# A graph kernel's edge stage: zeros written by ScalarE instead of GpSimd, target windows at fixed places, and later waits on VectorE and TensorE

## The chip, the cores and the metric

The kernel runs on one core of a Trainium2 chip. The metric is the device time of one execution in microseconds. Engines are named as the profile names them: PE is TensorE, DVE is VectorE, ACT is ScalarE, POOL is GpSimd and SP is SyncE, which here only issues transfers.

## The reference

Two graph networks run on 3,125 nodes of 128 features and 53,125 directed edges, sorted by target node. The first has one costly part, a three-layer network per edge, in both directions, with its sums per node:

```
edge_inputs  = concatenate([x[src], x[dst], edge_features])          # 3*128 wide
edge_states  = w3 @ relu(w2 @ relu(w1 @ edge_inputs + b1) + b2) + b3  # 384 -> 256 -> 256 -> 128
agg          = segment_sum(edge_states, dst)                          # and the same with src and dst exchanged
s1 = gru(x, agg); s2 = gru(agg, s1); s3 = gru(s1, s2); x = layernorm(x + s3)
for l in range(3):                                                    # second network
    X = relu(((1 + eps[l]) * X + segment_sum(X[src], dst)) @ W1[l] + b1[l]) @ W2[l] + b2[l]
x = layernorm(x + X)
```

The second network's segment sum is done as a product with a dense matrix of edge counts (3,125 x 3,125), which the edge stage counts on the way.

## The kernel before

The work has three stages: `edge_stage`, `gru_stage` and `sum_stage`. The change touches the first, which takes most of the time.

The edges are cut into G = 104 groups of 512. Because they are sorted by target, the 512 edges of a group have their targets in a short run of nodes. Each engine has its own program for a group, called a turn, and the engines meet at semaphores.

What a turn does, in the order of the data:

- POOL gathers the rows `x[src]` into `xg` (`gather`, L431), four transfers per group; SP loads the edge features `ef`, a copy of the group's indices in every partition (`rowb`), and a window of 128 node rows `xw`, whose first node `base` is read from a table `base_i` computed in the prologue from the group's smallest target.
- ACT rounds `xw` to `xwh` (`upper`, L573) and DVE takes the rest, `xwl` (L791). DVE makes the one-hot matrix `hot` (L806) and PE forms x[dst] as `xwh * hot + xwl * hot` (L1147, L1148). These two and the transposes of `xg` are `turn_sd`.
- ACT copies the transposed rows to `sd` (L554), DVE forms sum and difference (L786, L787), ACT rounds them (`upper_sd`, L559; `upper_e`, L567, for the features) and DVE takes the lower parts `sdl` (`lower_parts`, L796 and L799).
- PE does the first layer (`first`, L1106), ACT the bias (`pb`, L578), DVE the two directions (`ways`: `hpre`, L769 and L770), ACT the rounding with the relu (`h1h`, L584), DVE the lower parts `h1l` (L775). PE does the second layer (`second`, L1120), ACT its relu (L590), PE the third (`third`, L1131), ACT copies the two results to `es` (L598).
- `total` on PE sums the first direction into the group's window of 128 nodes (L1178, with the one-hot matrices `same[par][:, 0]` of `nodes`, L813) and combines equal indices of the second direction (L1183, with `same[par][:, 1]` of `compare`, L820). DVE adds the first to `aggt` at column `base` (`deliver`, L903). ACT copies the second to `outb` (L608), and POOL adds its rows to a table in HBM (`add`, L438), at places that DVE computes in `places` (L828 to L842).
- Beside this, DVE makes one-hot matrices of the edges' rows and columns (`pair_hot`, L874, L875), PE multiplies them (`pairs_of`, L1162) and DVE adds the counts to a band of the count matrix (`count_pairs`, L885, two halves per group). The `band` is a ring of three blocks of 120 columns; every fourth group one block is complete. SP then writes it to HBM (`flush`), POOL zeroes it (L462) and raises `s_fresh`, for which DVE waits at the head of the turn that will use it again. Every twelfth group DVE folds the ring's overhang back (`wrap`, L891, L893).

The order of instructions on each engine is written out by hand. The 12-turn loops of DVE, POOL and SP run seven rounds from group 8 (10 for SP), with the other groups before and behind them; PE and ACT loop over two turns. The prologue clears `aggt`, `band` and the later stage's `x1` on POOL (L422 to L424), computes per group the smallest and largest target and from these `base_i`, two ring places and a flag `fits`; if every group fits its windows, the windowed program runs, which is the case in the trace, else a general one.

## Time and profile before

| what | value |
|---|---|
| median of 3 runs | 2551.1 us (2547.54 to 2552.36) |
| profiled execution, its own time | 2548.59 us |
| its span in the profile | 2546.7 us |
| mean granted PE clock | 0.965 |
| PE busy | 2328.4 us, 91% of the span |
| DVE busy | 1831.1 us, 72% |
| ACT busy | 1145.7 us, 45% |
| POOL busy | 1269.6 us, 50% |

The own time is 1.9 us above the span, which leaves out what lies around it. The span falls into four stretches: the prologue to 42 us, the 104 groups from 42 to about 2050 us, the recurrent layers to 2223 us, and the three sum layers to the end. Busy shares tell little here, since PE is busy in most of every stretch; what matters is by how much a group takes longer than its PE work.

### The profile page before, as it was taken

The numbers are of one execution on the slowest core, as the hardware profiler recorded it, in microseconds if no ns is written. First come the engines' busy times: TensorE is split into PE (matmuls) and PEld (weight loads), VectorE is DVE, ScalarE is ACT, GpSimd is POOL, SyncE is SP. The second block draws the span as 40 slices with busy tenths as digits, with TensorE's granted clock in tenths as the row PEclk, the third lists the DMA queues.
The fourth block names the chain that finished last, engine by engine and source line by source line (L and its number), as shares of the span: only waits on it lengthen the run. The fifth ranks groups of instructions, "written<-read, shape, count | busy, mean of one in ns | idle before, by whom it ended". The sixth has DMA issues, their size and how long they took to land. (4 is left out here: it accounts for less than half of the span.)

```text
span 2546.7 us, 43212 instructions
## 1 busy us (share of the span) xinstructions
PE 2328.4 (91%) x12735; PEld 1942.8 (76%) x12735; DVE 1831.1 (72%) x3624; ACT 1145.7 (45%) x2031; POOL 1269.6 (50%) x873
## 2 busy tenths in 40 slices
PE   3999998999999999999999999999999949799997
PEld 2888787888778877878787788788887835478886
DVE  8888887888788877878887788778888836611114
ACT  1555555455455545545555455455555504311112
POOL 4566566666566666665665566556666410000000
PEclk9999999999999999999999999999999979899999
DMA  4356555355555355554355453555543462086963
GB/s 139 77 117 120 98 91 96 75 93 101 93 95 92 79 94 92 97 103 81 76 107 91 90 91 83 90 91 96 102 89 76 68 155 98 26 358 234 392 253 152
DMA packets 238770, 296.04 MB, mean 116 GB/s; under 512 B 125755, under 2 KB 196286, under 8 KB 230220
## 3 DMA queue, kind: packets, MB, share of 16 engines
q1 hardware_dynamic: 165449, 240.46, 33.9%
q0 software_dynamic: 73216, 54.58, 16.6%
q14 instruction: 89, 0.73, 0.1%
q8 instruction: 16, 0.26, 0.0%
HBM read 221.91 MB, written 73.05 MB: 116 GB/s over the span
## 5 line engine op out<-in xcount | busy, mean ns | idle before, releaser
L438 POOL DMA_INDIRECT sums<-outb,target x416 | 695.5, 1672 | 645.6 <-ACT outb L608 416.3
L431 POOL DMA_INDIRECT xg<-in_x,gidx x416 | 493.1, 1185 | 151.6 <-issue 135.8
L590 ACT ACTIVATE h<-ebank,b2c 128x512 f32<-128x512 f32 x416 | 286.7, 691 | 343.5 <-PE ebank L1120 343.5
L1131 PEld LDWEIGHTS ebank<-w3t,h 128*128 128x128 f32 x3328 | 403.9, 192 | 13.4
L1131 PE MATMUL ebank<-w3t,h 128*128 128x128 f32 x3328 | 404.7, 275 | 0.0
L1120 PE MATMUL ebank<-h1h,w2h 128*128 128x512 f32 x832 | 369.9, 445 | 3.9 <-DVE h1l L775 3.9
L1120 PE MATMUL ebank<-h1h,w2l 128*128 128x512 f32 x832 | 329.6, 396 | 0.0
L1120 PE MATMUL ebank<-h1l,w2h 128*128 128x512 f32 x832 | 329.2, 396 | 0.0
L584 ACT ACTIVATE h1h<-hpre 128x512 fp32r<-128x512 f32 x416 | 237.8, 622 | 125.8 <-DVE hpre L770 125.8
L1106 PE MATMUL ebank<-sdh,w1h 128*128 128x512 f32 x624 | 255.7, 410 | 39.0 <-DVE sdl L796 34.8
L775 DVE SCALAR_TENSOR_TENSOR h1l<-hpre,h1h 128x512 fp32r<-128x512 f32 x416 | 258.8, 679 | 0.0
L578 ACT ACTIVATE pb<-ebank,b1c 128x512 f32<-128x512 f32 x208 | 143.3, 689 | 245.1 <-PE ebank L1106 245.1
L1106 PE MATMUL ebank<-sdh,w1l 128*128 128x512 f32 x624 | 251.3, 403 | 0.0
L1106 PE MATMUL ebank<-sdl,w1h 128*128 128x512 f32 x624 | 249.9, 401 | 0.0
L875 DVE TENSOR_SCALAR colhot<-spots,colkey 128x500 bf16<-128x500 f16 x416 | 202.8, 487 | 0.0
L1120 PEld LDWEIGHTS ebank<-h1h,w2h 128*128 128x128 f32 x832 | 160.6, 193 | 38.7 <-DVE h1l L775 4.3
L1120 PEld LDWEIGHTS ebank<-h1h,w2l 128*128 128x128 f32 x832 | 158.6, 191 | 37.4
L1106 PEld LDWEIGHTS ebank<-sdh,w1h 128*128 128x128 f32 x624 | 121.3, 194 | 78.6 <-DVE sdl L796 41.2
L1120 PEld LDWEIGHTS ebank<-h1l,w2h 128*128 128x128 f32 x832 | 160.2, 193 | 25.4
L1178 PE MATMUL ebank<-same,es 128*128 128x128 f32 x832 | 119.0, 289 | 56.7 <-ACT es L598 56.7
L885 DVE TENSOR_TENSOR band<-band,ebank 128x500 f32 x208 | 139.9, 672 | 41.0 <-issue 31.3
L903 DVE TENSOR_TENSOR aggt<-aggt,ebank 128x128 f32 x104 | 30.0, 289 | 187.6 <-PE ebank L1178 125.8
(250 smaller groups left out, 4117.3 us busy)
## 6 DMA issues: line engine op xcount, KB each, us to landing
ring<-adj SPq DMA_DIRECT2D x54, 1568.0 KB, 8.1
rowb<-along SPq DMA_DIRECT2D x104, 512.0 KB
adj<-band SPq DMA_DIRECT2D x25, 1500.0 KB, 13.9
ef<-in_edge_attr SPq DMA_DIRECT2D x103, 256.0 KB, 2.7
stay<-adj SPq DMA_DIRECT2D x6, 1568.0 KB, 14.4
xg<-in_x,gidx POOLq DMA_INDIRECT x416
xw<-in_x SPq DMA_DIRECT2D x104, 64.0 KB
sums<-outb,target POOLq DMA_INDIRECT x416
```

The lines of the kernel that those rows point to most:

```text
L431: pool.indirect_dma_start(out=to, out_offset=None, in_=a["x"], in_offset=bass.IndirectOffsetOnAxis(ap=ids, axis=0)).then_inc(s_x[par], 16)
L438: pool.indirect_dma_start(out=tables[k % 2], out_offset=bass.IndirectOffsetOnAxis(ap=target[par][:, 1, k:k + 1], axis=0), in_=outb[par][:, ...
L578: nc.scalar.activation(pb[:, f, :], bank[2 + 2 * f][:, :], ACT.Identity, bias=b1c[:, f:f + 1]).then_inc(s_pc, 1)
L584: nc.scalar.activation(h1h[:, way, f, :], hpre[:, f, way, :], ACT.Relu).then_inc(s_h1, 1)
L590: nc.scalar.activation(h2[:, way, f, :], bank[6 + f][:, :], ACT.Relu, bias=b2c[:, f:f + 1]).then_inc(s_h2, 1)
L775: nc.vector.scalar_tensor_tensor(out=h1l[:, way, f, :], in0=hpre[:, f, way, :], scalar=0.0, in1=h1h[:, way, f, :].bitcast(fp32), op0=ALU.m ...
L875: last = nc.vector.tensor_scalar(colhot[:, t, :], spots[:, 0:WIDE], of(colkey, t), None, ALU.is_equal)
L885: nc.vector.tensor_tensor(part, part, bank[4 + half][:, 0:WIDE].rearrange("p (b c) -> p b c", c=WIN), ALU.add).then_inc(s_acc, 1)
L1106: last = nc.tensor.matmul(bank[bk + 2 * f][:, :], w[:, f, j, :], x[:, j, :], start=(q == 0), stop=(q == len(parts) - 1))
L1120: last = nc.tensor.matmul(bank[6 + f][:, :], w[:, f, k, :], h[:, way, k, :], start=(q == 0), stop=(q == len(parts) - 1))
L1131: last = nc.tensor.matmul(bank[6 + way][:, t * P:(t + 1) * P], h2[:, way, k, t * P:(t + 1) * P], w3t[:, k, :], start=False, stop=(t == K - ...
L1178: last = nc.tensor.matmul(bank[0][:, 0:P], es[:, 0, t * P:(t + 1) * P], same[par][:, 0, t, :], start=(t == 0), stop=(t == K - 1))
```

## The change

1. **Zeros.** POOL's three memsets of the prologue and its memset of a band block every fourth group go. DVE makes one row of 380 zeros (`none`). ACT copies it, broadcast, to `band`, `aggt` and `x1` at its start, and in the loop it clears a third of a block (25 x 40 columns) in each of the three turns before the block is used again, between `upper` and `first`. For this ACT's loop becomes one of 12 turns, and POOL's, which has no events any more, one of 2 turns. `s_fresh` counts thirds.
2. **Fixed windows.** Group g's window of target nodes begins at `30 g - 16` (clamped at both ends) and is 80 wide (`SPAN`), in place of a computed place and 128. `base_i` shrinks to the two ring places (`slot_i`); SP and DVE no longer load a base from it. `hot`, `xw`, `xwh`, `xwl` use 80 partitions, the node matrices (`into`) 80 columns, L1178 80 moving columns. `fits` also asks that every group's targets lie in its window.
3. **Order and waits.** In DVE's turn `nodes` comes ahead of the first `count_pairs`, the wait for `s_fresh` stands behind `sums` and `nodes`, the second `count_pairs` stands behind `lower_parts`, the wrap stands behind it and one turn earlier, and `places` stands ahead of `deliver`. PE waits for the counts (`s_acc`) ahead of the second half of `first` only.

```diff
-            nc.gpsimd.memset(aggt[:, :], 0.0)
-            nc.gpsimd.memset(band[:, :], 0.0).then_inc(s_band, 1)
-            nc.gpsimd.memset(later.x1[:, :, :], 0.0).then_inc(later.s_zero, 1)
...
-                    if event:
-                        i, b = event
-                        pool.wait_ge(s_flush, i * 16)
-                        plain()
-                        nc.gpsimd.memset(band_of(slots(b), slots(b) + BLK), 0.0).then_inc(s_fresh, 1)
...
+                def clear(i, b, third):
+
+                    act.wait_ge(s_flush, i * 16)
+                    lo = slots(b) + third * (BLK // 3)
+                    nc.scalar.copy(band_of(lo, lo + BLK // 3), none[:, 0:BLK // 3].unsqueeze(1)
+                                   .broadcast_to([P, NB, BLK // 3])).then_inc(s_fresh, 1)
+
...
+                    if cleared:
+                        clear(*cleared)
                     if ahead:
                         first(g + 1)
...
+                    with act.Fori(0, ROUNDS) as m:
+                        for q in range(12):
+                            turn(m * 12 + (8 + q), q % 2, m * 6 + (4 + q // 2),
+                                 cleared=(m * 3 + (2 + q // 4), q // 4, q % 4 - 1) if q % 4 else None)
...
+            nc.scalar.copy(band[:, :].rearrange("p (b c) -> p b c", c=BAND),
+                           none[:, :].unsqueeze(1).broadcast_to([P, NB, BAND])).then_inc(s_band, 1)
...
-                    base = dve.value_load(base_i[0:1, bass.ds(g * 4, 1)], min_val=0, max_val=N - P)
-                    part = aggt[:, bass.ds(base, P)]
-                    nc.vector.tensor_tensor(part, part, bank[0][:, 0:P], ALU.add).then_inc(s_agg, 1)
+                    part = aggt[:, bass.ds(first_node(g), SPAN)]
+                    nc.vector.tensor_tensor(part, part, bank[0][:, 0:SPAN], ALU.add).then_inc(s_agg, 1)
 
                 def turn(g, par, turns, ahead=2, early=0, fresh=None, wrapped=None):
+                    begin = isinstance(g, int) and g == 0
+                    if ahead:
+                        sums(g + 1)
+                    if begin:
+                        pair_keys()
+                        pair_hot(0)
+                    if ahead:
+                        nodes(g + 1, 1 - par, early=early == 2)
                     if fresh is not None:
                         dve.wait_ge(s_fresh, fresh)
-                    if ahead:
-                        sums(g + 1)
-                    if isinstance(g, int) and g == 0:
-                        pair_keys()
-                        pair_hot(0)
-                    if wrapped is not None:
-                        dve.wait_ge(s_acc, g * 2)
-                        wrap(wrapped)
-                    if not (isinstance(g, int) and g == 0):
+                    if not begin:
                         count_pairs(g, 0)
                     if ahead:
-                        nodes(g + 1, 1 - par, early=early == 2)
-                    if not (isinstance(g, int) and g == 0):
-                        count_pairs(g, 1)
-                    if ahead:
                         lower_parts(g + 1)
...
+                    count_pairs(g, 1)
+                    if wrapped is not None:
+                        dve.wait_ge(s_acc, g * 2 + 2)
+                        wrap(wrapped)
+                    if ahead:
+                        compare(g + 1, 1 - par, turns + par)
                     if ahead == 2:
                         onehot(g + 2, par, turns + 1)
                         window(g + 2, par)
                     if ahead:
                         pair_hot(g + 1)
                         ways(g + 1)
+                        places(g + 1, 1 - par, early=early == 2)
                     deliver(g)
-                    if ahead:
-                        places(g + 1, 1 - par, early=early == 2)
```

The first place is DVE's program inside its loop, from the add of the sums to `compare`. The names are those of the list above; `s_aT` says that PE has the pair products, `s_acc` that a half was counted. Before:

```order
L786 TENSOR_TENSOR sd<-sd,ebank 128x512 [waits s_sdT]
L787 TENSOR_TENSOR sd<-sd,ebank 128x512
...
L885 TENSOR_TENSOR band<-band,ebank 128x25x20
L813 ISA [waits s_sum]
L813 TENSOR_TENSOR same<-column,inwin 128x512
...
L885 TENSOR_TENSOR band<-band,ebank 128x25x20
L795 REGISTER_ALU
L796 TENSOR_TENSOR sdl<-ebank,sdh 128x512 [waits s_hi]
L799 TENSOR_TENSOR sdl<-sd,sdh 128x1024 [waits s_hi]
L820 ISA [waits s_rowb0]
L820 TENSOR_TENSOR same<-rowb,keys 128x512
```

The same place of the changed kernel, whose line numbers are some 30 higher (L816 is L786 of before, L915 is L885, L826 and L829 are L796 and L799, L850 is L820):

```order
L816 TENSOR_TENSOR sd<-sd,ebank 128x512 [waits s_sdT]
L817 TENSOR_TENSOR sd<-sd,ebank 128x512
L843 ISA [waits s_sum]
L843 TENSOR_TENSOR into<-column,inwin 128x320
...
L915 TENSOR_TENSOR band<-band,ebank 128x25x20
L825 REGISTER_ALU
L826 TENSOR_TENSOR sdl<-ebank,sdh 128x512 [waits s_hi]
L829 TENSOR_TENSOR sdl<-sd,sdh 128x1024 [waits s_hi]
...
L915 TENSOR_TENSOR band<-band,ebank 128x25x20
L850 ISA [waits s_rowb0]
L850 TENSOR_TENSOR same<-rowb,keys 128x512
```

One count has moved from ahead of the lower parts to between them and the comparison, and the node matrix is narrower.

The second place is the end of DVE's turn, behind `ways`. Before:

```order
L775 SCALAR_TENSOR_TENSOR h1l<-hpre,h1h 128x512 [waits s_h1]
L901 ISA [waits s_agg,s_sum]
L901 TENSOR_LOAD base_i
L901 ISA x2
L903 ISA
L903 TENSOR_TENSOR aggt<-aggt,ebank 128x128
L828 TENSOR_TENSOR match<-same,lower 128x512 [waits s_cmp]
...
L842 TENSOR_TENSOR target<-shift,keys 128x4 [waits s_cs]
```

And in the changed kernel:

```order
L805 SCALAR_TENSOR_TENSOR h1l<-hpre,h1h 128x512 [waits s_h1]
L858 TENSOR_TENSOR match<-same,lower 128x512 [waits s_cmp]
...
L871 REGISTER_ALU [waits s_add1,s_add0]
L872 TENSOR_TENSOR target<-shift,keys 128x4 [waits s_cs]
L932 ISA [waits s_agg,s_sum]
L932 TENSOR_TENSOR aggt<-aggt,ebank 128x80
```

The target computation now stands ahead of the delivery, with its wait for POOL's adds (`s_add0`, `s_add1`), and the load of a base is gone.

The third place is ACT's program in its new loop, in a turn that clears a third of a block; before, the turn had the same rows without the clear.

```order
L573 CAST xwh<-xw 80x128 [waits s_sdT]
L612 ISA
L614 COPY band<-none 128x25x40 [waits s_flush]
L578 ACTIVATE pb<-ebank,b1c 128x512 [waits s_p]
L577 REGISTER_ALU
L578 ACTIVATE pb<-ebank,b1c 128x512 [waits s_p]
```

The clear stands between the window's rounding and the first layer's bias.

## Rows read from the trace of the kernel before

**Rows 1.** Windows, L1147 to next: length, PE, PEld, DVE, ACT, POOL, clock, DMA.
```profile
98.84:116.58 17.74, 17.74 (x110) 15.15 (x108) 15.03 (x32) 10.15 (x18) 10.66 (x9) 1.00 0.38 79
169.76:191.62 21.86, 19.57 (x109) 16.68 (x108) 18.02 (x33) 10.03 (x18) 15.73 (x10) 0.92 0.85 170
284.47:304.35 19.88, 18.28 (x109) 14.99 (x108) 16.01 (x33) 10.13 (x18) 10.75 (x8) 1.00 0.52 95
322.08:342.45 20.37, 17.95 (x110) 15.18 (x108) 18.12 (x32) 10.04 (x18) 12.95 (x9) 1.00 0.34 68
435.33:459.31 23.98, 19.79 (x109) 16.01 (x108) 14.94 (x32) 10.02 (x18) 10.40 (x8) 0.93 0.49 81
```

**Rows 2.** One line, once per group: PE's first product of `turn_sd`; first and last start.
```profile
L1147 PE MATMUL ebank<-hot,xwh x104: 474/478/776, 42.0 to 2019.6; 128*128 128x512 f32 x104
```

**Rows 3.** One line: POOL's memset of a band block, min/median/max in ns.
```profile
L462 POOL MEMSET band<- x24: 3188/3195/3203, 177.6 to 1954.0; 128x3000 f32 x24
```

**Rows 4.** Timeline of DVE while a memset runs (177.59 to 180.8): start, length.
```profile
177.25 3.58 DVE L874 TENSOR_SCALAR rowhot<-spots,rowkey 128x128 bf16<-128x128 f16 x1
```

**Rows 5.** Waits of PE: for whom, us in total, times, longest.
```profile
PE ebank L1178 <- ACT es L598: 56.7, 24, 2.5
```

**Rows 6.** Window right behind such a wait; the number behind POOL's is PE's clock.
```profile
186.00:190.00 4.00, 3.63 (x18) 3.54 (x19) 2.29 (x5) 1.00 (x3) 1.89 (x1) 0.61 1.13 145
```

**Rows 7.** Timeline of the prologue.
```profile
2.86 13.36 DVE L674 CAST column<-count_i 128x128 f32<-128x128 int32 x1 [0.43 <-POOL lower L420]
...
3.87 0.25 SPq L251 DMA_DIRECT2D pb<-in_dst  x1
...
13.38 2.76 POOL L424 MEMSET x<- 128x3200 f32 x1
...
17.79 0.69 DVE L689 CAST hpre<-pb 104x1024 f32<-104x1024 int32 x1
...
34.93 0.30 ACT L573 CAST xwh<-xw 128x128 fp32r<-128x128 f32 x1 [4.76 <-DMA xw<-in_x]
```

**Rows 8.** Transfers of the first 45 us: count, size, us to landing.
```profile
ef<-in_edge_attr SPq DMA_DIRECT2D x3, 256.0 KB, 2.6
```

**Rows 9.** Timeline of one group, from the lower parts to `total`.
```profile
365.42 1.21 DVE L799 TENSOR_TENSOR sdl<-sd,sdh 128x1024 fp32r<-128x1024 f32 x1
...
367.77 0.69 ACT L578 ACTIVATE pb<-ebank,b1c 128x512 f32<-128x512 f32 x1 [0.51 <-PE ebank L1106]
...
369.94 0.67 DVE L769 TENSOR_TENSOR hpre<-pb,ebank 128x512 f32<-128x512 f32 x1
...
373.49 0.57 ACT L598 COPY es<-ebank 128x512 f32<-128x512 f32 x1
...
374.24 0.97 PEld L1178 LDWEIGHTS ebank<-same,es 128*128 128x128 f32 x8
...
374.55 0.59 ACT L598 COPY es<-ebank 128x512 f32<-128x512 f32 x1 [0.49 <-PE ebank L1131]
```

**Rows 10.** First `es` and L1178 in another group.
```profile
1013.64 0.57 ACT L598 COPY es<-ebank 128x512 f32<-128x512 f32 x1
...
1014.88 0.97 PEld L1178 LDWEIGHTS ebank<-same,es 128*128 128x128 f32 x8
```

**Rows 11.** Timeline at the DVE loop's second round: ACT's last copy, then DVE's first work.
```profile
433.86 0.59 ACT L608 COPY outb<-ebank 128x512 f32<-128x512 f32 x1 [1.32 <-PE ebank L1183]
...
441.57 0.69 DVE L786 TENSOR_TENSOR sd<-sd,ebank 128x512 f32<-128x512 f32 x1 [5.58 <-issue]
```

**Rows 12.** Timeline of DVE in a turn with a wrap.
```profile
286.95 0.67 DVE L891 TENSOR_TENSOR band<-band 128x500 f32<-128x500 f32 x1
...
289.16 0.68 DVE L885 TENSOR_TENSOR band<-band,ebank 128x500 f32 x1 [0.89 <-DVE band L893]
```

**Rows 13.** Groups of instructions: busy us, mean ns.
```profile
L559 ACT CAST sdh<-sd 128x1024 fp32r<-128x1024 f32 x104 | 110.1, 1059 | 17.1 <-DVE sd L787 17.1
L1178 PE MATMUL ebank<-same,es 128*128 128x128 f32 x832 | 119.0, 289 | 56.7 <-ACT es L598 56.7
```

More of the change, by code:

```diff
@@ L57 @@
 ROUNDS = 7
+PACE = 30
+BACK = 16
+SPAN = 80
+NB_A = 16
 assert G == 4 * ITERS and WIDE <= 512
@@ L127, in edge_stage @@
         rowb = [sb(f"rowb{i}", [P, 2, GE]) for i in range(2)]
-        same = [sb(f"same{i}", [P, 2, K, P]) for i in range(2)]
+        same = [sb(f"same{i}", [P, K, P]) for i in range(2)]
+        into = [sb(f"into{i}", [P, K, SPAN]) for i in range(2)]
+        none = sb("none", [P, BAND])
         target = [sb(f"target{i}", [P, 3, K], i32) for i in range(2)]
@@ L470, in windowed @@
                 for j in range(1, 8):
-                    turn(j, j % 2, j // 2, event=(1, -1) if j == 6 else None)
-                with pool.Fori(0, ROUNDS) as m:
-                    for q in range(12):
-                        turn(m * 12 + (8 + q), q % 2, m * 6 + (4 + q // 2),
-                             event=(m * 3 + (2 + q // 4), q // 4) if q % 4 == 2 else None)
-                for j in range(8 + 12 * ROUNDS, G + 1):
-                    turn(j, j % 2, j // 2, gathers=("last" if j == G - 3 else j < G - 3),
-                         event=(j // 4, j // 4 - 2) if j % 4 == 2 and j // 4 < ITERS - 1 else None)
+                    turn(j, j % 2, j // 2)
+                with pool.Fori(4, (G - 4) // 2) as i:
+                    for par in range(2):
+                        turn(i * 2 + par, par, i)
+                for j in range(G - 4, G + 1):
+                    turn(j, j % 2, j // 2, gathers=("last" if j == G - 3 else j < G - 3))
                 for t in range(2):
@@ L641, in program @@
                 first(0)
[L642 to L648 removed]
+                if win:
+                    for g in range(8):
+                        turn(g, g % 2, g // 2, early=g < 2, cleared=(1, -1, g % 4 - 1) if g > 4 else None)
+                    with act.Fori(0, ROUNDS) as m:
+                        for q in range(12):
+                            turn(m * 12 + (8 + q), q % 2, m * 6 + (4 + q // 2),
+                                 cleared=(m * 3 + (2 + q // 4), q // 4, q % 4 - 1) if q % 4 else None)
+                    for g in range(8 + 12 * ROUNDS, G):
+                        turn(g, g % 2, g // 2, ahead=min(2, G - 1 - g),
+                             cleared=(g // 4, g // 4 - 2, g % 4 - 1) if g % 4 and g // 4 < ITERS - 1 else None)
+                else:
+                    turn(0, 0, 0, early=True)
+                    turn(1, 1, 0, early=True)
+                    with act.Fori(1, (G - 2) // 2) as i:
+                        for par in range(2):
+                            turn(i * 2 + par, par, i)
+                    turn(G - 2, 0, 0, ahead=1)
+                    turn(G - 1, 1, 0, ahead=0)
+            act.wait_ge(s_none, 1)
+            nc.scalar.copy(band[:, :].rearrange("p (b c) -> p b c", c=BAND),
+                           none[:, :].unsqueeze(1).broadcast_to([P, NB, BAND])).then_inc(s_band, 1)
+            nc.scalar.copy(aggt[:, :].rearrange("p (b c) -> p b c", c=AW // NB_A),
+                           none[:, 0:AW // NB_A].unsqueeze(1).broadcast_to([P, NB_A, AW // NB_A])).then_inc(s_band, 1)
+            nc.scalar.copy(later.x1[:, :, :], none[:, 0:D].unsqueeze(1).broadcast_to([P, NB, D])).then_inc(later.s_zero, 1)
             act.wait_ge(s_wload, 6 * 16)
@@ L1095, in _, with first @@
             pe.wait_ge(s_fits, 1)
-            def first(g, start=False):
+            def first(g, start=False, pairs=False):
                 if not start:
```

98 lines of the change are left out of this document (48 added, 50 removed).

## The prediction

> **What bounds the kernel now.** The busy shares come first: PE is busy in 91% of the span, so its work sets the floor, and the question is what each of the 104 groups takes above it. The windows from one group's L1147 to the next answer that. An undisturbed group takes 17.74 us with PE busy throughout [rows 1]. The 104 stand from 42.0 to 2019.6 [rows 2], 103 steps of 19.2 us; 103 times 17.74 would be 1827, so 150 us are lost in disturbed groups. Stepping through them I find three recurring kinds, of which the windows show samples: groups in which POOL clears a band block (24: 18 lose about 4.1 us, 6 about 2.6, together 90), groups with a wrap (8, mostly 2.1, together 20) and groups at DVE's loop edge (6, 4.8 to 6.6, together 36) [rows 1].
>
> The clearing groups: a memset takes 3.19 us, 24 times [rows 3]. While one runs, to 180.8, DVE's small `rowhot` takes 3.58 us and ends with it [rows 4]: DVE is held. The delay runs through `hpre` and `h1h` to ACT's `es`, and PE waits for that ahead of L1178, 24 times, 2.4 us each [rows 5]. Behind such a wait the granted clock is 0.61 in a window of 4 us [rows 6], so part of it runs at the lower of the two levels, 1.2 GHz. That makes the 4.1; where a group loses only 2.6, the clock stayed at 1.00 [rows 1].
>
> The prologue shows the same hold: DVE's cast of 128x128 takes 13.36 us, to 16.22, and POOL's third memset ends at 16.14 [rows 7].
>
> **The change part by part.** *Prologue.* Nothing holds the casts now. From their end to L689 the chain took 1.6 us (16.2 to 17.8), eight steps of 0.2. The casts begin at 2.9; with an estimated 0.8 for both, the same 1.6, and 1.0 for five new steps they end at 6.3. The last index load is issued at 3.87 [rows 7]; transfers land after 2.6 us [rows 8], at 6.5. So L689 stands near 6.5 in place of 17.79: 11.3. The copy of `base_f`, the clamp and `wnode` leave the path behind it, four short steps, 0.7: **-12**. ACT's three copies have 15,836 columns at 1.03 ns (1.059 us for 1,024 [rows 13]), 16.4 us from about 3 on. ACT's first work for a group, at 34.93 before [rows 7], comes at 23, so they are hidden; at 25% slower they would touch it. Bounds: -9 to -13.
>
> *Band clears.* POOL's memsets leave the loop, and with them the loss of the 24 groups: **-90**. ACT makes 72 copies of 1,000 columns instead, 1.03 us each by the same row, 74 us. What hides them is ACT's slack ahead of `pb`: it waits 0.51 us there, so `pb` comes 0.5 later; `pb` ends at 368.46 and `hpre`, which reads it, starts at 369.94, 1.5 us on [rows 9]. The `flush` that a clear waits for is issued over a turn earlier. Cost 0; without that cover 0.5 us in 72 turns, 37.
>
> *DVE's order.* L799 waits for ACT's rounding, so what stood ahead of it in DVE's queue was nearly free, and what stands behind isn't. The second count moves behind it, 0.68 us [rows 12], 0.6 as a step of the queue, on the path L799, L820, `pair_hot`, `hpre`, `h1h`, `es`. `es` comes 0.5 to 0.6 later. Is there room? In the group at 360 us the first `es` ends at 374.06 and L1178's weights load at 374.24, 0.18 us [rows 9]; in the one at 1000 us it ends at 1014.21 against 1014.88, 0.67 us [rows 10]. The odd groups look like the first, the even ones like the second. I take 0.3 us for half the groups and nothing for the rest, 16; the bounds are 0 and 0.6 in each, 60.
>
> *80 columns.* The narrower `nodes` and the value loads saved lie ahead of the wait for ACT: 0. L1178 takes 119.0 us in all [rows 13], and at 80 of 128 columns could save 45. But L1183 behind it waits for the second `es`, which ends at 375.14, and L1178's loads end at 375.21 [rows 9]; made faster, PE would wait instead: 0. It only softens the late first `es`, by nothing to all of the 16; I take a fifth, since its loads stay 128 columns wide: **+13** for both. The Trainium skill ("TensorE: Matmul & The Clock Gate", LDWEIGHTS) gives a weight load as P / 1.2 ns for P columns, 107 ns here. L1178's eight loads take 0.97 us, 121 each [rows 9], near it; by the rule nothing is softened, +16.
>
> *`places` ahead of `deliver`.* It fills time in which DVE waited for PE's sum, and I put `deliver`'s end just ahead of PE's next `turn_sd`. It waits for POOL's adds, with `deliver` behind it and PE behind that. POOL is idle 7 of an undisturbed group's 17.7 us [rows 1], so the adds should be in time. Cost 0.
>
> *Wrap.* From L891 to the count behind it 2.2 us passed [rows 12]. Now no count waits there: about 1.5 to `compare`, which delays `hpre` and not L796. 8 times 0.6, **-5**.
>
> *Loop edges.* DVE is idle for 5.58 us, for nothing that the profile shows [rows 11], at each of the six returns of its 12-turn loop (4.4 to 5.8). That stays, and ACT, whose two-turn loop shows no such gap, gets a loop of 12 turns, some 350 instructions against DVE's 800. I expect a gap on ACT too. Its last copy ends at 434.45; 5.5 us later it is 440, and after `h` and `sd`, 0.6 each, 441.2: DVE came back at 441.57 [rows 11]. The gaps overlap, and these groups lose what they lost: **-2**. The Trainium skill ("Runtime: NRT & Kernel Launch", Instruction fetch mechanics) says that a taken branch to a target outside the two pages held stalls an engine for a fetch. DVE's gaps agree; for ACT the rule is why I expect one.
>
> **Sum.** -12 -90 +13 -5 -2 = -96 against the profiled execution's own 2548.6: 2452.6. The median stood 2.5 above that: **2455**.
>
> **The rivals.** *Order costs more.* POOL's transfers hold DVE more once `pair_hot` comes later, and each group loses 0.5 to 0.6 us: +55 for +13, 2497. For it: two undisturbed groups already differ by 0.49 us in slack [rows 9, 10]. *ACT is a second late engine.* Clears not hidden (37) or edges 4 us longer each (24): 2480 to 2490. Against it: `pb`'s 1.5 us of room. *More is gained.* The narrow L1178 softens all, and the edges shrink by DVE's earlier start: 2436. *Slower than before.* `target` waits for POOL's adds, `deliver` stands behind it, PE's `turn_sd` behind that. The place is the end of each turn, the price the adds' lateness beyond their room, for which I take half of POOL's idle 7 us. From 0.9 us beyond it, in all 104 groups, the 96 us are gone; at 1.5, 2611. Against it: half the room is much. *The windows don't fit* and the general program runs: excluded by the seeded edges, whose targets lie 0 to 79 nodes above the fixed place in all 104 groups, just inside the 80.
>
> **How the numbers follow.** Forecast, 2440 to 2470: 0.6. Order costs more, 2470 to 2515: 0.15. ACT late, 2470 to 2492: 0.1. More gained, 2425 to 2440: 0.1. Slower: 0.03. No change, by a mixture: 0.02. 2433 to 2495 leaves out half of the case below the forecast and a third of the first above it, 0.05 each, and the last two, 0.05: 0.15 in all. Under 0.2% (5 us) nothing can be told from no change here. Faster 0.95, same 0.02, slower 0.03.
>
> **What would show it.** The prologue's cast at 0.3 us and PE's first L1147 near 30. No waits of 2.4 us of L1178 for `es`; short ones, under 0.6, in odd groups. Clears near 1.03 us. A gap of 4 to 6 us on ACT at six places beside DVE's. The prediction fails if waits for `sdl`, `aggt` or `target` turn up in most groups, if the undisturbed step lies outside 17.7 to 18.1, or if the clock is low as often as before.

## The result, and the profile after

The changed kernel takes 2452.3 us in the median (2447.8 to 2455.4), beside 2551.7 us for the kernel before on the same chip; the ratio is 0.959, with a 95% interval of 0.957 to 0.962. Its profiled execution took 2454.33 us with a span of 2452.2 us, at a mean granted PE clock of 0.977 where it was 0.965. The forecast was 2455.

To see where the time went I took from both traces the start of PE's first matmul of `turn_sd` in each of the 104 groups (L1147 before, L1178 now), and sorted the 103 steps between them by the kinds that the prediction named. The floor is the median step times 103; what stands behind it is the excess over that.

| us | before | after | forecast change | change |
|---|---|---|---|---|
| first matmul of `turn_sd` | 42.0 | 30.1 | -12 | -11.8 |
| floor, 103 steps of 17.74 and 17.88 | 1827.2 | 1841.6 | +13 | +14.4 |
| 24 clearing groups | 90.3 | -0.1 | -90 | -90.4 |
| 8 wrap groups | 20.1 | 11.6 | -5 | -8.5 |
| 6 edge groups | 36.0 | 35.2 | -2 | -0.8 |
| first two steps | 3.7 | 3.6 | 0 | -0.1 |
| all other steps | 0.4 | 3.8 | 0 | +3.4 |
| last such matmul to the end | 527.1 | 526.3 | 0 | -0.8 |
| span | 2546.7 | 2452.2 | -96 | -94.5 |

The windows of the trace after, one group each, answer to those of before [rows 1]: two plain groups, one with a clear, one with a wrap, one at the loop edge, and the one step that stands out by itself.

```profile
87.38:105.24 17.86, 17.86 (x110) 15.14 (x107) 14.32 (x31) 10.04 (x18) 13.33 (x9) 1.00 0.39 77
105.24:123.11 17.87, 17.87 (x109) 15.13 (x108) 14.25 (x31) 10.03 (x18) 13.23 (x9) 1.00 0.68 120
289.11:307.01 17.90, 17.90 (x109) 15.16 (x108) 14.42 (x31) 10.86 (x19) 14.69 (x9) 1.00 0.36 79
251.95:271.23 19.28, 18.07 (x110) 15.17 (x108) 15.56 (x33) 10.73 (x19) 14.94 (x9) 1.00 0.73 125
414.35:439.02 24.67, 19.60 (x110) 16.31 (x108) 14.42 (x31) 10.33 (x18) 10.90 (x9) 0.93 0.51 82
194.59:216.16 21.57, 18.09 (x109) 15.06 (x108) 14.31 (x31) 10.66 (x18) 12.14 (x9) 1.00 0.78 107
```

A group with a clear (the third line) takes what a plain one takes, and its clock is whole. The plain step itself has grown from 17.74 to 17.87, with PE busy throughout: PE doesn't wait, it works longer.

The prologue in the timeline (start, duration, engine, line): the cast that had taken 13.36 us [rows 7] takes 0.23.

```profile
2.11 8.11 ACT L671 COPY band<-none 128x9500 f32<-128x9500 f32 x1
2.80 0.23 DVE L701 CAST column<-count_i 128x128 f32<-128x128 int32 x1
6.25 0.69 DVE L722 CAST hpre<-pb 104x1024 f32<-104x1024 int32 x1 [0.67 <-DMA pb<-in_dst]
12.83 2.85 ACT L675 COPY x<-none 128x3200 f32<-128x3200 f32 x1
25.23 0.30 ACT L573 CAST xwh<-xw 80x128 fp32r<-80x128 f32 x1 [9.55 <-DMA xw<-in_x]
30.12 0.78 PE L1178 MATMUL ebank<-hot,xwh 80*128 80x512 f32 x1
```

L722 (L689 before) starts at 6.25 where 6.5 was worked out, now behind a transfer, and ACT's copies end at 15.68, nine and a half microseconds ahead of ACT's first work for a group.

A clearing group on its way from the clear to PE, in the timeline:

```profile
296.17 1.03 ACT L614 COPY band<-none 128x1000 f32<-128x1000 f32 x1
297.10 0.68 ACT L578 ACTIVATE pb<-ebank,b1c 128x512 f32<-128x512 f32 x1
298.98 0.67 DVE L799 TENSOR_TENSOR hpre<-pb,ebank 128x512 f32<-128x512 f32 x1
302.53 0.57 ACT L598 COPY es<-ebank 128x512 f32<-128x512 f32 x1
303.32 0.97 PEld L1209 LDWEIGHTS ebank<-into,es 128*128 128x128 f32 x8
```

`pb` ends at 297.78, `hpre` starts 1.2 us later, and the first `es` ends at 303.10, 0.22 us ahead of the loads of L1209 (L1178 before). The room is small, and the clear doesn't use it up. In the list of waits (us in total, times, longest):

```profile
PE ebank L1209 <- ACT es L598: 10.6, 9, 1.4
PE ebank L1098 <- ACT sd L554: 25.3, 6, 5.1
ACT h L590 <- issue: 40.8, 6, 7.6
```

The 24 waits of 2.4 us [rows 5] are gone; nine of up to 1.4 are left, and eight of them stand in the groups with a wrap. The last line is new: ACT stands still for 6.8 us on average, six times, at the return of its 12-turn loop. At the first of them the timeline shows who waits for whom:

```profile
421.11 0.69 ACT L590 ACTIVATE h<-ebank,b2c 128x512 f32<-128x512 f32 x1 [7.64 <-issue]
422.40 1.11 PE L1098 MATMUL ebank<-ident,ef 128*128 128x128 f32 x4 [5.07 <-ACT sd L554]
422.41 0.69 DVE L816 TENSOR_TENSOR sd<-sd,ebank 128x512 f32<-128x512 f32 x1 [9.09 <-ACT sd L554]
```

DVE's own gap, which ended last before [rows 11], can't be seen by itself any more: DVE's first row waits 9.09 us, and what ends that is ACT's `sd`. So if the gap is still there it lies inside ACT's. That fits the forecast of an overlap, since the six groups lose what they lost, but ACT is the one that ends it.

The step of 21.57 us is one that the prediction had as the mechanism of its rival *Slower than before*:

```profile
215.14 0.16 DVE L872 TENSOR_TENSOR target<-shift,keys 128x4 int32<-128x4 f32 x1 [4.29 <-DMA sums<-outb,target]
215.37 0.24 DVE L932 TENSOR_TENSOR aggt<-aggt,ebank 128x80 f32 x1
215.75 0.65 PE L1098 MATMUL ebank<-ident,xg 128*128 128x128 f32 x4 [3.48 <-DVE aggt L932]
```

`target` waits for GpSimd's adds, `deliver` (L932) stands behind it, and PE behind that. It happens once in this trace, for 3.5 us, in a window whose DMA share is 0.78, and not in the other groups. It isn't chance either. Seven traces of the experiments have `places` ahead of `deliver` and leave PE's waits as changed, and in each of them the adds are late in this same group, the tenth: `target` waits 2.3 to 4.3 us and PE then 1.5 to 3.8. In the kernel before and in `clears_alone` neither wait is there.

### The profile page after: what moved, and what is told of

Read it like the earlier page. It is cut to its first block and busy times, and to the rows that moved or that the text cites. A ratio compares the mean times of both kernels' runs of the same rounds, so it can differ in the third digit from the quotient of the medians.

```text
span 2452.2 us, 42170 instructions
## 1 busy us (share of the span) xinstructions
PE 2299.6 (94%) x12735; PEld 1915.7 (78%) x12735; DVE 1702.2 (69%) x3628; ACT 1220.9 (50%) x2106; POOL 1333.8 (54%) x846
## 5 line engine op out<-in xcount | busy, mean ns | idle before, releaser
L445 POOL DMA_INDIRECT sums<-outb,target x416 | 675.2, 1623 | 477.4 <-ACT outb L608 225.3
L438 POOL DMA_INDIRECT xg<-in_x,gidx x416 | 653.9, 1572 | 160.7 <-issue 140.6
L1137 PE MATMUL ebank<-sdh,w1h 128*128 128x512 f32 x624 | 247.6, 397 | 2.1 <-DVE sdl L826 1.5
L816 DVE TENSOR_TENSOR sd<-sd,ebank 128x512 f32<-128x512 f32 x104 | 71.6, 688 | 256.0 <-ACT sd L554 252.2
L1794 DVE TENSOR_TENSOR xl<-xb,xh 128x128 fp32r<-128x128 f32 x75 | 21.7, 292 | 187.4 <-ACT xh L1759 186.5
L598 ACT COPY es<-ebank 128x512 f32<-128x512 f32 x208 | 118.8, 576 | 57.6 <-PE ebank L1162 57.6
L829 DVE TENSOR_TENSOR sdl<-sd,sdh 128x1024 fp32r<-128x1024 f32 x104 | 127.4, 1225 | 24.9 <-ACT sdh L559 24.5
L799 DVE TENSOR_TENSOR hpre<-pb,ebank 128x512 f32<-128x512 f32 x208 | 140.6, 676 | 4.5 <-ACT pb L578 2.1
## 6 DMA issues: line engine op xcount, KB each, us to landing
stay<-adj SPq DMA_DIRECT2D x6, 1568.0 KB, 14.4
```

Of the source, the lines that this page charges most:

```text
L438: pool.indirect_dma_start(out=to, out_offset=None, in_=a["x"], in_offset=bass.IndirectOffsetOnAxis(ap=ids, axis=0)).then_inc(s_x[par], 16)
L445: pool.indirect_dma_start(out=tables[k % 2], out_offset=bass.IndirectOffsetOnAxis(ap=target[par][:, 1, k:k + 1], axis=0), in_=outb[par][:, ...
L799: nc.vector.tensor_tensor(hpre[:, f, 0, :], pb[:, f, :], bank[3 + 2 * f][:, :], ALU.add)
L829: nc.vector.tensor_tensor(sdl[:, 0:2, :], sd[:, :, :, :].rearrange("p s k d -> p s (k d)"), sdh[:, 0:2, :].bitcast(fp32), ALU.subtract).th ...
L1137: last = nc.tensor.matmul(bank[bk + 2 * f][:, :], w[:, f, j, :], x[:, j, :], start=(q == 0), stop=(q == len(parts) - 1))
```

## The experiments

Each ratio is to the kernel before on the chip of that run. The chips differ (the kernel before took 2557, 2569 and 2557 us on the three of the experiments), so the ratios and the steps in the traces are compared, and times only where the runs shared a chip; the absolute times in the expectations are on the scale of the first chip. The runs of `start_alone`, `clears_alone`, `old_order` and `wide_windows` shared one; `late_wait`, `shifted`, `early_wait` and `written_out` a second; the last four a third.

### What made the gain

**start_alone**: the kernel before, with these three copies ahead of ACT's program in place of GpSimd's three start-up memsets; DVE makes the row of zeros.

```diff
-            nc.gpsimd.memset(aggt[:, :], 0.0)
-            nc.gpsimd.memset(band[:, :], 0.0).then_inc(s_band, 1)
-            nc.gpsimd.memset(later.x1[:, :, :], 0.0).then_inc(later.s_zero, 1)
...
+            nc.scalar.copy(band[:, :].rearrange("p (b c) -> p b c", c=BAND),
+                           none[:, :].unsqueeze(1).broadcast_to([P, NB, BAND])).then_inc(s_band, 1)
+            nc.scalar.copy(aggt[:, :].rearrange("p (b c) -> p b c", c=AW // NB_A),
+                           none[:, 0:AW // NB_A].unsqueeze(1).broadcast_to([P, NB_A, AW // NB_A])).then_inc(s_band, 1)
+            nc.scalar.copy(later.x1[:, :, :], none[:, 0:D].unsqueeze(1).broadcast_to([P, NB, D])).then_inc(later.s_zero, 1)
```

> The kernel before, with only the start-up clears of the arrays moved to ACT (the memsets of the band in the loop stay on GpSimd). If the hold of DVE by GpSimd's start-up memsets is the whole of the prologue's gain: the cast of 128x128 takes about 0.3 us in place of 13.36, PE's first matmul of turn_sd stands near 30 in place of 42, the steps of the groups stay those of before, and the time is 12 us under the kernel before, about 2540. If ACT's three copies stand in the way of what they replaced, less than 9 us is gained, 2543 or more.

Measured: 2544.5 us beside 2557.1, ratio 0.996 (0.994 to 0.998), 12.6 us less. In its timeline:

```profile
2.78 0.23 DVE L681 CAST column<-count_i 128x128 f32<-128x128 int32 x1
30.53 0.78 PE L1155 MATMUL ebank<-hot,xwh 128*128 128x512 f32 x1
```

The clearing groups still lose 89.5 us. The first theory holds: the term is -12, and the fixed windows, which aren't in this kernel, have little part in it (30.5 here, 30.1 in the changed kernel).

**clears_alone**: all clears on ACT, with its loop of 12 turns; DVE's order, the windows and PE's waits as before.

```diff
-                        nc.gpsimd.memset(band_of(slots(b), slots(b) + BLK), 0.0).then_inc(s_fresh, 1)
...
+                    if cleared:
+                        clear(*cleared)
...
-                             fresh=m * 3 + (1 + q // 4) if q % 4 == 0 else None, wrapped=m if q == 4 else None)
+                             fresh=m * 9 + (q // 4 + 1) * 3 if q % 4 == 0 else None, wrapped=m if q == 4 else None)
```

> The kernel before, with every clear on ACT (start-up and loop, ACT's loop of 12 turns), and nothing else of the change: DVE's order, the 128-node windows at loaded places and PE's waits are those of before. Theory A, the prediction's sum: -12 and -90 and nothing for the edges, about 2449, and the undisturbed step stays 17.74 us; what the changed kernel has above 17.74 (its undisturbed step is 17.88) comes from the other parts. Theory B: the clears on ACT and its longer loop bring the 0.14 us per group themselves: step 17.88, about 2461. Theory C, part of the gain came from DVE's order: some groups behind a clear still lose 1 us or more, above 2465.

Measured: 2444.7 us beside 2557.1, ratio 0.957 (0.954 to 0.960). The windows of a plain group and of one with a wrap:

```profile
87.75:105.49 17.74, 17.74 (x109) 15.15 (x108) 14.68 (x32) 10.05 (x18) 11.93 (x9) 1.00 0.39 79
265.07:284.79 19.72, 18.28 (x109) 15.00 (x108) 16.21 (x34) 10.04 (x18) 10.74 (x8) 1.00 0.56 98
```

Theory A. The clears alone bring all of the gain, at a span (2445.3 us) below that of the changed kernel; the undisturbed step stays at 17.73. By the two traces the rest of the change together costs some 7 us: 15 of floor and 3 in other steps, less 4 in the wraps, 4 at the edges and 3 in what is left. The timed ratios, 0.957 and 0.959, lie the same way, with intervals that overlap.

**unused_memset**: is it the memset beside DVE, or something that waited for it? This is the changed kernel with four memsets of an unused tile in every fourth turn of POOL. Here nobody waits.

```diff
+                        if q == 2:
+                            for c in range(4):
+                                nc.gpsimd.memset(unused[:, :], 0.0).then_inc(s_unused, 1)
+                                pool.wait_ge(s_unused, i * 4 + (c - 7))
+                                plain()
```

> The changed kernel with GpSimd memsets put back that nothing depends on: every fourth turn, behind its adds, four memsets of 750 columns, 3000 in all as in the kernel before, into an unused tile; nobody waits for them. ACT's clears stay. Theory, the memsets hold DVE and that alone made the losses: DVE's rowhot and colhot stretch to 1 us and more beside them, those groups lose 2 to 4 us again, 23 times, 2500 to 2540. Rival, what was lost before was a wait for the cleared band or for a late GpSimd: about 2455, with no stretched rowhot. The new tile moves sdh to 448 modulo 512: if only the address modulo 64 matters (0, as in the changed kernel) the undisturbed step is 17.88 us, if modulo 512 it is 17.73 us.

Measured: 2504.9 us, ratio 0.980 (0.977 to 0.982), 50 us above the changed kernel on the same chip. In the timeline of one of these groups:

```profile
472.46 0.83 DVE L911 TENSOR_SCALAR rowhot<-spots,rowkey 128x128 bf16<-128x128 f16 x1
472.52 0.73 POOL L481 MEMSET unused<- 128x750 f32 x1 [0.15 <-POOL unused L481]
473.35 0.83 DVE L911 TENSOR_SCALAR rowhot<-spots,rowkey 128x128 bf16<-128x128 f16 x1
473.40 0.72 POOL L481 MEMSET unused<- 128x750 f32 x1 [0.15 <-POOL unused L481]
478.81 1.12 PE L1216 MATMUL ebank<-into,es 128*128 128x80 f32 x8 [1.67 <-ACT es L605]
```

`rowhot`, 0.24 us by itself, takes 0.83 beside a memset of 0.72, and PE waits 1.67 us for `es` in the end. The 23 groups lose 51.5 us: 17 lose 1.7 to 2.1, six 3.3 to 3.6. The theory holds, with a stretch a little under the 1 us that it named: a memset on GpSimd that nothing depends on costs PE time through DVE. The rule of the Trainium skill ("SBUF — State Buffer", Who interferes with whom) is that `tensor_scalar` in a 2-port mode and GpSimd take one shared pair of ports whole, each for the length of its instruction; `rowhot` at 0.83 us beside a memset of 0.72 agrees. Which mode `rowhot` ran in, no run here shows. That it is 51 and not 90 may lie in the shorter memsets, between which DVE gets instructions through; that wasn't tried apart.

**whole_block**: one copy of 3000 columns in one turn.

```diff
-                    lo = slots(b) + third * (BLK // 3)
-                    nc.scalar.copy(band_of(lo, lo + BLK // 3), none[:, 0:BLK // 3].unsqueeze(1)
-                                   .broadcast_to([P, NB, BLK // 3])).then_inc(s_fresh, 1)
+                    if third:
+                        return
...
+                    nc.scalar.copy(band_of(slots(b), slots(b) + BLK), none[:, 0:BLK].unsqueeze(1)
+                                   .broadcast_to([P, NB, BLK])).then_inc(s_fresh, 1)
```

> The changed kernel with each band block cleared by one ACT copy of 3000 columns in one turn in place of three of 1000 in three turns. It tests the cover of the clears. A copy of 3000 columns takes 2.6 us, so pb's first half starts at 9.6 us after turn_sd's matmul in place of 7.96, and hpre, which starts at 9.83 now, at 10.4 or later: es comes 0.6 to 1.0 us later where 0.2 is free, 24 groups lose 0.4 to 0.8 and up to 1.7 more where the clock drops: 2463 to 2500. If ACT had far more room than the prediction took: 2453. If a clear of any size delays PE one for one: each group loses 1.6 and more, 2492 or above.

Measured: 2466.0 us, ratio 0.963 (0.961 to 0.966), 11 us above the changed kernel on the same chip (8 by the spans).

```profile
292.53 2.71 ACT L615 COPY band<-none 128x3000 f32<-128x3000 f32 x1
295.14 1.25 ACT L578 ACTIVATE pb<-ebank,b1c 128x512 f32<-128x512 f32 x2
300.12 1.09 PE L1210 MATMUL ebank<-into,es 128*128 128x80 f32 x8 [0.17 <-ACT es L598]
```

Each of the 24 groups takes 18.24 in place of 17.88, 0.36 us, and none loses clock. So ACT has 1.0 us free for certain and, of the 1.7 us more, pays 0.36. The cover that the prediction claimed is there, and thirds are within it; the cost of a whole block was a little under the small end of what I expected (0.4).

### Where the step of 17.88 us comes from

The prediction had a late first `es` in every odd group. The trace shows the same +0.14 in odd and even groups, with no wait. Timeline rows, first of the changed kernel, then of clears_alone: the first two of the 18 matmuls of `first()`, and the one behind them.

```profile
93.42 0.40 PE L1137 MATMUL ebank<-sdh,w1h 128*128 128x512 f32 x1
93.66 0.39 PE L1137 MATMUL ebank<-sdl,w1h 128*128 128x512 f32 x1
97.62 0.40 PE L1158 MATMUL ebank<-b3hl,ones_r 128*128 128x512 f32 x1
```

```profile
93.75 0.39 PE L1127 MATMUL ebank<-sdh,w1h 128*128 128x512 f32 x1
93.98 0.39 PE L1127 MATMUL ebank<-sdl,w1h 128*128 128x512 f32 x1
97.87 0.40 PE L1148 MATMUL ebank<-b3hl,ones_r 128*128 128x512 f32 x1
```

18 matmuls take 4.20 us in one and 4.12 in the other, 0.233 and 0.229 each, at a granted clock of 1.00 in both. `second()` differs in the same way (12 of its matmuls 2.88 and 2.84 us); the third layer's matmuls, of 128 moving columns, don't (16 take 1.70 us in both). Four runs look for the cause.

**old_order**: the changed kernel with DVE's `turn` of before.

```diff
-                        lower_parts(g + 1)
-                    count_pairs(g, 1)
+                    count_pairs(g, 1)
+                    if ahead:
+                        lower_parts(g + 1)
...
-                        places(g + 1, 1 - par, early=early == 2)
                     deliver(g)
+                    if ahead:
+                        places(g + 1, 1 - par, early=early == 2)
```

> The changed kernel with DVE's order of before: second count ahead of the rounding's lower parts, wait for the clears at the head of the turn, wrap a turn later ahead of the counts, places behind deliver. If DVE's order costs the 0.14 us that the undisturbed step has gained: step 17.74, about 2452 - 13 + 6 for the wraps, 2445. If the order costs nothing: step stays at 17.88, the wrap groups lose 2.1 us again and not 1.5, about 2457.

Measured: 2450.7 us beside 2557.1, ratio 0.959 (0.957 to 0.962); step 17.87 to 17.90, wraps 1.93 us over it on average in place of 1.45 (15.4 us in all, not 11.6). DVE's order isn't the cause, and costs nothing in the floor.

What the order does move is `es`. In the group of old_order that answers to the clearing group shown above, whose first matmul stands at 285.65, the first `es` and the loads that need it are these:

```profile
298.57 0.57 ACT L598 COPY es<-ebank 128x512 f32<-128x512 f32 x1
299.85 0.97 PEld L1210 LDWEIGHTS ebank<-into,es 128*128 128x128 f32 x8
```

`es` ends 13.49 us into the group and 0.71 us ahead of the loads. In the changed kernel it ends 13.99 us into the group (303.10 against 289.11) and 0.22 ahead. So the new order makes `es` 0.5 us later, as the prediction said, and what that uses up is room and not time.

**wide_windows**: the changed kernel with `SPAN = 128`.

> The changed kernel with windows of 128 nodes at the same fixed places in place of 80 (also 128 rows of weights and 128 rows moved in the two matmuls of turn_sd, and 128 moved columns in total). If the 80-wide shapes cost the 0.14 us of the step: step 17.74, about 2440. If they have no part in it: step 17.88 and 2452. If they soften a late es, as the prediction took: step 17.95 or more in odd groups, 2455 to 2465.

Measured: 2454.2 us beside 2557.1, ratio 0.961 (0.958 to 0.963); step 17.88 to 17.90. The narrow shapes aren't the cause, and they soften nothing that matters: odd groups take 17.90 in the median with 128 columns too, and the whole floor is 2 us longer. The loads of the narrow L1209 take 0.97 us for eight, as before [rows 9].

**late_wait**: clears_alone, with PE's wait for the counts inside `first()`.

```diff
                 for f in range(HB):
+                    if pairs and f == 1:
+                        pe.wait_ge(s_acc, g * 2)
...
-                        pe.wait_ge(s_acc, (g + 1) * 2)
-                        first(g + 1)
+                        first(g + 1, pairs=True)
```

> The kernel with only the clears moved (clears_alone), and PE's wait for the first pair count moved as in the changed kernel, into first(), between its two halves of w1. DVE's order is that of before, so the count is there early and the wait never waits. The step of the undisturbed groups was 17.73 us without it and is 17.89 in the three kernels with it, whose matmuls of 512 columns follow each other at 0.233 us in place of 0.229. Theory A, the placed wait slows PE's stream: step 17.88, 2445 + 14 = 2459. Theory B, the cause is elsewhere (where the tiles lie in SBUF, see the next run): step 17.73, 2445.

Measured: 2471.9 us beside 2568.8, ratio 0.962 (0.960 to 0.963). Windows of a plain group and of one with a wrap, and a row of the latter:

```profile
85.55:103.28 17.73, 17.73 (x109) 15.14 (x108) 14.96 (x32) 10.05 (x18) 10.92 (x9) 1.00 0.38 79
493.56:514.78 21.22, 18.51 (x109) 15.02 (x108) 16.49 (x36) 10.05 (x18) 11.07 (x8) 1.00 0.57 93
```

```profile
511.40 0.59 ACT L591 COPY es<-ebank 128x512 f32<-128x512 f32 x1 [1.91 <-remote]
```

The step is 17.73: theory A of the step falls. But neither theory foresaw that the 103 steps together are 26 us longer than in clears_alone. It isn't in the plain groups: the wraps lose 27.8 us in place of 15.8, ten other groups 0.5 to 4 each, the edges 4 more. In every wrap group ACT's second `es` comes 1.5 us later, behind something that the profile has no name for, and PE waits for it. The changed kernel has no such row and loses 11.6 us in its wraps. I can't say what it is; it stays open. The chip may have a part in it. By the timed ratios, 0.962 and 0.957, late_wait is only 13 us worse than clears_alone, and its trace has idle time that clears_alone's lacks (under **shifted**).

**shifted**: the changed kernel with an unused tile.

```diff
+        pad = sb("pad", [P, 312])
         gidx = [sb(f"gidx{i}", [P, 2, K], i32) for i in range(3)]
```

> The changed kernel with one unused tile of 1248 bytes ahead of gidx, so that every tile behind it, those that PE reads among them, lies at the address modulo 512 that it has in the kernel before (sdh: 224; in the changed kernel 0, since diag and the table of places became smaller). Nothing else differs. Theory B, the addresses set the pitch of the matmuls: step 17.73 to 17.75 us in place of 17.88, about 2453 - 14 = 2439. Theory A, PE's wait: 17.88 and 2453.

Measured: 2455.2 us beside 2568.8, ratio 0.956 (0.9545 to 0.9574). Windows of a plain group and of the first edge:

```profile
85.20:102.91 17.71, 17.71 (x110) 15.14 (x108) 14.26 (x31) 10.04 (x18) 13.17 (x9) 1.00 0.37 78
413.07:439.00 25.93, 20.12 (x109) 16.76 (x108) 14.30 (x31) 10.32 (x18) 10.78 (x8) 0.87 0.52 83
```

Theory B: the step is 17.72 with nothing changed but where the tiles lie. The floor falls by 15.4 us. In this one profile that is given back, 9 us at the edges (44.2 in place of 35.2, with the clock at 0.87 in the window above where it was 0.93) and 6 in other groups, so that its span is 2452.7. The timed ratio is lower than the changed kernel's by 0.3%, with intervals that overlap.

Whether the shifted tiles did that is doubtful. In this trace ACT stands still again and again for nothing that the profile shows. Two of its waits, and one of written_out's below:

```profile
ACT h L591 <- issue: 91.4, 50, 8.4
ACT h1h L585 <- issue: 66.2, 62, 2.5
ACT h1h L584 <- issue: 55.2, 63, 2.5
```

Counting stretches of over 0.5 us in the 104 groups, without the six at the loop's return, ACT has 119 of them in shifted, 105 in written_out, 55 in early_wait and 35 in late_wait. These are the four runs of the second chip. The ten other traces have at most one each, out_and_shifted among them, which has the same tiles as shifted. So they go with that chip, as far as these runs tell, and what the traces of late_wait and shifted lose outside the plain groups may be its doing. No kernel was traced on that chip and on another, which would decide it.

The sums of what stands ahead of `sdh` give its address in each kernel: 224 modulo 512 in the kernel before, start_alone, clears_alone, late_wait and shifted, all with a step of 17.73; 0 in the changed kernel, old_order and wide_windows, and 448 in unused_memset, all with 17.86 to 17.90. Modulo 64 that is 32 for the fast ones and 0 for the slow ones. The weights of the three layers stand ahead of `gidx` and lie at one address in all of them, so of what the slowed matmuls read only the moving side has moved. Of the tiles behind `gidx` all move together, so which of them matters isn't told apart.

### What holds the late wait of PE in place

**early_wait**: the changed kernel with PE's wait ahead of `first()`.

> The changed kernel with PE's wait for the pair counts ahead of first() again, as before. DVE's second count ends at 6.97 us after turn_sd's matmul and PE wants to begin first() at 6.05, so every group waits some 0.9 us there if nothing else gives way: step 18.8, 2453 + 90 = 2543, nearly the time before. If theory A of the step holds as well, 0.14 less each, 2530. If the count comes earlier by itself (DVE waits for ACT less), 2500. Not slower than 2460 would mean that the wait didn't need to move.

Measured: 2560.5 us beside 2568.8, ratio 0.997 (0.995 to 0.998); step 18.98. In the timeline of one group, DVE's second count and PE's first matmul of `first()`:

```profile
97.01 0.67 DVE L915 TENSOR_TENSOR band<-band,ebank 128x500 f32 x1
97.78 0.47 PE L1137 MATMUL ebank<-sdh,w1h 128*128 128x512 f32 x1 [0.86 <-DVE sdl L829]
```

The count ends at 97.68 and PE starts 0.1 us behind it. The row names `sdl`; what had really been missing is the count, by its end. The forecast of 0.9 us per group was 0.2 short. DVE's new order without PE's later wait would have given back nearly all of the gain. The two belong together.

### A version beyond both

**written_out**: the changed kernel with both 12-turn loops in straight code.

```diff
-                    with act.Fori(0, ROUNDS) as m:
+                    for m in range(ROUNDS):
...
-                with dve.Fori(0, ROUNDS) as m:
+                for m in range(ROUNDS):
```

> The changed kernel with ACT's and DVE's loops of 12 turns written out, 84 turns each in straight code. If the 6 us at each of the six edges are the fetch of code after the jump back, as the idle time that nothing in the profile explains suggests: the six edge groups fall from 23.7 to 17.9 us, 35 us less, about 2418, and no new gaps. Rival: straight code of that length is fetched late too, and the gaps come back as often or oftener, 2440 to 2500.

Measured: 2416.7 us beside 2568.8, ratio 0.941 (0.939 to 0.942); 38 us under shifted on the same chip. A window of the group that was the first edge:

```profile
413.89:431.78 17.89, 17.89 (x110) 15.15 (x108) 14.25 (x31) 10.05 (x18) 10.75 (x7) 1.00 0.71 102
```

The six edges lose nothing (24.67 us before), and the groups of the 84 straight turns take what they took. Of the two theories the first. ACT's own row of work isn't without gaps in this trace: it has the 105 short ones told under **shifted**, 98.7 us in all, which plain groups hide. They don't come from straight code, since out_and_shifted has the same loops written out and none of them.

**after_again** and **out_and_shifted**: the changed kernel once more, and written_out with the tile of shifted.

> The changed kernel itself, on the same chip as the other three, so that small differences can be told: ratio to the kernel before 0.955 to 0.962, step 17.88 us, gaps of 23 to 25 us at six edges.

> The changed kernel with both loops written out (written_out) and the tiles moved by 1248 bytes (shifted). The gain of the shifted tiles was given back in the groups around the loop edges (24.6 to 25.9 us in place of 22.9 to 24.7). Without edges: step 17.73, 33 us less for the edges and 10 to 14 less for the steps than the changed kernel on the same chip, about 1.8% less. If the gain is given back elsewhere (a late es that the slower matmuls hid): steps of 17.8 to 18.2 in many groups and no better than written_out, 1.4% less.

Measured: after_again 2454.9 us beside 2557.2, ratio 0.959 (0.957 to 0.961), with edges of 22.9 to 25.3 us. out_and_shifted 2404.0 us on the same chip, ratio 0.939 (0.937 to 0.941), 51 us or 2.1% under after_again.

```profile
86.59:104.30 17.71, 17.71 (x109) 15.14 (x108) 14.32 (x31) 10.04 (x18) 13.74 (x9) 1.00 0.39 78
408.99:426.84 17.85, 17.85 (x109) 15.17 (x108) 14.54 (x31) 10.05 (x18) 11.76 (x6) 1.00 0.69 102
```

Of the 50.6 us between the two spans the floor has 16.4 and the edges 36.3; 2 us come back, in the first two steps. Without edges, and on a chip whose traces lack ACT's short gaps, the shifted tiles pay in full. Which of the two was missing in shifted isn't told apart. It is the fastest version here.

## Why the prediction was right, step by step

*Prologue*, -12: -11.8 in the trace, -12.6 alone. Right, down to L722 at 6.25 where 6.5 was worked out. ACT's copies were sized 3 us too long (13.6 us, not 16.4): a long one takes 0.85 us per 1,000 columns, not 1.03. They are hidden at either rate.

*Band clears*, -90 and no cost on ACT: -90.4. Right. Its mechanism, that a memset holds DVE and that nobody need wait for it, is shown in kind by unused_memset, which brings back 51 of the 90 us; clears_alone shows that all 90 go with the memsets. The cover of the 72 copies is shown by whole_block.

*DVE's order with 80 columns*, +13: the floor rose by 14.4, but not in the way forecast. `es` does come 0.5 us later by the order, as worked out (old_order). The step that failed is the room ahead of L1178. I took the 0.18 us of the group at 360 us [rows 9] for a trait of all odd groups that the change would leave alone. In the kernel before, the first `es` ends 13.39 us into a plain even group and 13.87 into a plain odd one, in the median; in clears_alone, with the same order, 13.38 and 13.37. So the short room of the odd groups went away when the clears left GpSimd. Both kinds then had 0.66 us, and in the changed kernel 0.27 and 0.23 are left: PE waits nowhere in a plain group, and with old_order the step is the same to 0.02 us. The order costs nothing. What costs is the place of the tiles in SBUF, through the time between PE's matmuls; shifted undoes it. The sum came out right by luck, because a cost that I didn't know had the size of one that wasn't there. The softening by narrow windows, 3 of its 16 us, had nothing to soften (wide_windows). The rule of the Trainium skill ("TensorE: Matmul & The Clock Gate", LDWEIGHTS) on weight loads, by which the term was +16, decides nothing here: the loads of L1209 are as long as those of L1178 were (0.97 us for eight), but no `es` of a plain group is late for them to make up.

*`places` ahead of `deliver`*, 0: nearly right. In one group the adds are late and PE pays 3.5 us; in after_again it is the same group and 1.5 us. It is the mechanism of the rival *Slower than before*, at one place in 104 that comes back in every such trace, and the prediction put nothing there. In the other groups the adds are in time. Behind `deliver` they wouldn't be free either: in old_order they are as late (4.08 us) one group earlier, and that step is 2.2 us longer. Why they are late there stays open.

*Wrap*, -5: -8.5. The 0.6 us per wrap was right for six of the eight, which went from about 2.1 us to 1.45. The term left out the two others: they cost 3.75 us before, with the granted clock at 0.92 in their windows, and now cost 1.5 and 1.6. From clears_alone 4.3 of the 8.5 come without DVE's new order.

*Loop edges*, -2: -0.8, with the mechanism as forecast. ACT does get a gap, of 5.9 to 7.6 us where 4 to 6 was forecast and DVE had 4.4 to 5.8, and ends last in each of the six. The rule of the Trainium skill ("Runtime: NRT & Kernel Launch", Instruction fetch mechanics), that a taken branch to a target outside the two pages held stalls an engine for a fetch, agrees with ACT's gaps and with their going away in straight code.

*The rivals.* *Order costs more* is out: floor the same with either order. *ACT is a second late engine* is out for the clears, and for the edges it is true in kind and free in price. *More is gained* is out in the change as made; some 7 us of it were there to be had by the traces (clears_alone), by another way than it named. *Slower* happened at one place. The short waits for `es` in odd groups, named as a sign, didn't come.

## What to carry to other kernels

A large memset on GpSimd beside small DVE instructions can cost what DVE then owes to others, even when nobody waits for the memset: look for short DVE rows that end together with a GpSimd row. Read the floor of a stage as well as its waits: if the step of undisturbed groups moves while PE stays busy, look at the pitch of its matmuls and at what moved in SBUF, not at the queues. A loop body of 12 turns had a price at each return, on DVE and on ACT; where the two returned together the group paid no more than for one, and straight code paid nothing. Before an odd loss in one trace is put down to the kernel, see whether every trace of that chip has it.

## What the hardware showed that I had not expected

- The time between two matmuls of 512 columns was 0.229 us or 0.233 us at the same granted clock, by where the tiles lie: 17.73 us per group in the six kernels with `sdh` at 224 modulo 512, 17.88 in the six with 0 or 448 in which PE waits for nothing in plain groups. Which tile matters, and why, isn't shown.
- ACT's gap at the return of its loop was longer (5.9 to 7.6 us) than DVE's (4.4 to 5.8), though ACT runs fewer instructions (2106 counted in the profile of the changed kernel, DVE 3628).
- 84 turns of straight code on DVE and ACT lost nothing where the loops had lost 35 us, and fetched less: the queue of instruction transfers has 75 packets in written_out, 113 in the changed kernel, 89 in the kernel before.
- ACT copied 9,500 columns in 8.11 us and 1,000 in 1.03, 0.85 and 1.03 ns each.
